# Moving the routing steps, the first expert splits and the expert loads inside the key phase of a cross-attention and expert kernel

## What is computed

```python
x = x + fake_quant_matmul(layernorm(x), ctx)        # L0: quantised product with the context
x = x + moe(layernorm(x))                            # L0: 16 experts, 2 of 16 per token, and a shared pair
x = x + cross_attention(layernorm(x), ctx)           # L1: 32 query heads, 8 key/value heads of 128
x = x + gated_low_rank(layernorm(x))                 # L1: 64 experts of rank 8, 16 of 64 per token

# in moe():
scores = softmax(xt @ router_w + router_b) + router_bias
keep   = the 2 best of 4 groups by their best score
idx    = the 2 best experts among the kept groups
y      = sum over experts of gate[e] * ((silu(xt @ w1 + b1) * (xt @ w2 + b2)) @ w3 + b3)

# in cross_attention():
k = rmsnorm((ctx @ k_proj_w.T) per head); v = ctx @ v_proj_w.T    # k and v depend on ctx alone
```

## Time and profile before

| quantity | value |
|---|---|
| time, median of 3 executions | 661.31 us |
| lowest and highest of them | 659.51 and 673.06 us |
| the profiled execution (one of the three) | 673.06 us |
| its span, first to last instruction | 671.2 us |
| busy PE, DVE, ACT, POOL | 575.7, 458.4, 352.6, 366.9 us |
| chain that ended last: PE, POOL, DVE | 39%, 18%, 15% of the span |
| mean granted clock of TensorE | 0.954 |

### The profile page before, as it was taken

The page is one execution under the profiler, slowest core; times in us unless marked ns, Lnnn a source line. Parts: engine busy times, 40 slices in busy tenths (PEclk is TensorE's granted clock), DMA queues, the critical chain, the costliest instruction groups (busy, mean ns, idle before and its releaser), DMA issues.

```text
span 671.2 us, 11710 instructions
## 1 busy us (share of the span) xinstructions
PE 575.7 (86%) x3255; PEld 280.2 (42%) x3255; DVE 458.4 (68%) x1066; ACT 352.6 (53%) x792; POOL 366.9 (55%) x396
## 2 busy tenths in 40 slices
PE   2949967678676994999996899999999969999997
PEld 1414523376554443444441344444444424444453
DVE  6898698847777476555557999999999920000773
ACT  4336623546555404757566677777777723133132
POOL 5960137859898460678785444444545414368011
PEclk9979977879999996999998999999999979999999
DMA  9993027789987650487759999999999993324001
GB/s 343 408 372 132 17 49 195 149 277 329 361 285 255 217 176 1 109 196 181 204 111 200 180 171 179 179 184 178 180 184 177 179 160 118 125 73 178 1 1 63
DMA packets 211846, 118.78 MB, mean 177 GB/s; under 512 B 188497, under 2 KB 196817, under 8 KB 208866
## 3 DMA queue, kind: packets, MB, share of 16 engines
q1 hardware_dynamic: 209346, 108.58, 62.9%
q0 software_dynamic: 2288, 9.70, 4.7%
q10 hardware_dynamic: 176, 0.04, 0.0%
HBM read 56.94 MB, written 15.20 MB: 107 GB/s over the span
## 4 chain that ended last, share of the span: by engine, by line
PE 39%; POOL 18%; DVE 15%; issue 11%; SPq 7%; DMA 6%; ACT 3%; POOLq 0%; DVEq 0%; ACTq 0%
PE ps L345 12%; PE ps L347 12%; PE ps L346 12%; SPq L499 7%; POOL wsp L1292 6%; POOL hlr L1292 4%; POOL q_sb L1292 3%; DVE q_sb L1554 2%; PE ps L526 1%; POOL q_sb L1309 1%; DVE f32r L1707 1%; DMA stage<-in_moe,disp 1%; POOL hsp L1292 1%; DVE x_sb L1810 1%; DMA stage<-in_first_chunks 1%
## 5 line engine op out<-in xcount | busy, mean ns | idle before, releaser
L1292 POOL TENSOR_TENSOR wsp<-stage,wsp 128x512 f16<-128x512 f32 (+1 forms) x69 | 78.1, 1157 | 63.3 <-ACT wsp L1135 63.2
L1162 ACT ACTIVATE f32r<-f32r,mneg 128x512 f32<-128x512 f32 x128 | 91.4, 715 | 29.7 <-DVE mneg L1832 29.6
L1832 DVE CUSTOM_DVE_ANT_0 f32r<-ps,nmask 128x512 f32<-128x512 f32 x128 | 82.5, 680 | 1.9
L1427 POOL TENSOR_SCALAR hlr<-f32r,rinv 128x512 f16<-128x512 f32 x64 | 45.1, 714 | 47.6 <-DVE rinv L1837 45.9
L1427 POOL TENSOR_SCALAR stage<-f32r,rinv 128x512 f16<-128x512 f32 x64 | 43.6, 691 | 46.4 <-DVE rinv L1837 46.3
L1292 POOL TENSOR_TENSOR hlr<-f32r,hlr 128x512 f16<-128x512 f32 x36 | 41.2, 1155 | 48.1 <-ACT hlr L1244 33.5
L345 PE MATMUL ps<-q_sb 128*128 128x512 f16 x132 | 53.3, 404 | 15.5 <-POOL q_sb L1292 11.8
L1694 DVE TENSOR_REDUCE ss<-f32r 128x4 f32<-128x512 f32 x48 | 32.8, 684 | 47.1 <-ACT f32r L1045 47.0
L345 PE MATMUL ps<-k_sb,q_sb 128*128 (+1 forms) x128 | 49.4, 386 | 11.5 <-DVE mneg L1832 8.8
L346 PE MATMUL ps<-q_sb 128*128 128x512 f16 x132 | 53.2, 403 | 0.0
L347 PE MATMUL ps<-q_sb 128*128 128x512 f16 x132 | 52.7, 399 | 0.0
(11 more groups left out here) (363 smaller groups left out, 1539.7 us busy)
## 6 DMA issues: line engine op xcount, KB each, us to landing
stage<-in_wq SPq DMA_DIRECT2D x8, 1024.0 KB, 5.0
stage<-in_wo SPq DMA_DIRECT2D x8, 1024.0 KB, 4.7
q_sb<-in_moe SPq DMA_DIRECT2D x9, 768.0 KB, 7.6
xs_dram<-zeros SPq DMA_DIRECT2D x1, 5888.0 KB, 29.2
pT<-xs_dram SPq DMA_DIRECT2D x23, 256.0 KB, 6.2
r_dram<-f32r SPq DMA_DIRECT2D x23, 256.0 KB, 6.0
stage<-in_moe SPq DMA_DIRECT2D x6, 768.0 KB, 8.7
k_sb<-in_wkv SPq DMA_DIRECT2D x3, 1024.0 KB, 19.0
```

The lines of the kernel that those rows point to most:

```text
L1162: act.activation(f32r[:, j % 4, :], f32r[:, j % 4, :], ACT.Exp, bias=mneg[:, j % 4:j % 4 + 1], scale=-1.0, accum_out=psum_col[:, j % 4:j % ...
L1292: return pool.tensor_tensor(dst_lo, src, dst_hi, ALU.subtract)
L1427: pool.tensor_scalar(halves(j)[:, 0, :], f32r[:, j % 4, :], rinv[:, 0, j % 4:j % 4 + 1], PSCALE, ALU.mult, ALU.mult).then_inc(s_ph, 1)
L1832: dve.tensor_tensor_reduce(f32r[:, j % 4, :], ps[j % 4][:, :], nmask[:, qt, :], 0.125, BIG, ALU.add, ALU.min, mneg[:, j % 4:j % 4 + 1]).th ...
```

## The change

Five moves, and one size. (1) POOL makes the low halves of experts 0 and 1 and of the bias directly before the key phase instead of at tiles 11 to 15. (2) POOL's scatters stand at tiles 9 to 12 instead of 6 to 9. (3) PE's `positions` stands at tile 8 instead of 6, DVE's `slot_numbers` at 6 instead of 5 and `owners_and_gates` at 9 instead of 8. (4) SP loads experts 5, 2, 3 and 4 after the transposes of tiles 3 to 6 instead of before the phase, and experts 6 and 7 after tiles 7 and 8 instead of after tile 15. (5) SP loads the first four token blocks after tile 12 instead of 11. The size is `dynamic_dma_scratch_size`, the bytes of each SBUF partition set aside for the descriptors of POOL's DMAs, 1024 instead of 4096.

```diff
@@ sync
-            load_expert(5)
-            sp.wait_ge(s_cq, BATCH)
-            load_expert(2)
-            load_expert(3)
-            sp.wait_ge(s_vp, NST)
-            load_expert(4)
...
             for r in range(2 * NST):
                 k_transpose(r)
-                if r == 11:
+                if r == 3:
+                    load_expert(5)
+                if r == 4:
+                    sp.wait_ge(s_cq, BATCH)
+                    load_expert(2)
+                if r == 5:
+                    load_expert(3)
+                if r == 6:
+                    sp.wait_ge(s_vp, NST)
+                    load_expert(4)
+                if r in (7, 8):
+                    load_expert(r - 1)
+                if r == 12:
                     sp.wait_ge(s_disp, 1)
                     sp.wait_ge(s_sct, 16 * 2 * NT)
                     for n in range(4):
                         load_slots(n)
-            for n in (6, 7):
-                load_expert(n)
@@ tensor, beside_keys
-                if j == 6:
+                if j == 8:
                     positions()
@@ gpsimd
+            w12_lo(0)
+            w12_lo(1)
+            for n in range(2):
                 pool.wait_ge(s_w3h, n + 1)
                 low(split_at(n, 1, W3), landed_at(n, W3), split_at(n, 0, W3)).then_inc(s_w3p, 1)
-            def beside_keys(r):
-
-                if 6 <= r < 10:
-                    scatters(r)
-                elif r in (11, 13):
-                    w12_lo((r - 11) // 2)
-                elif r in (12, 14):
-                    w3_lo((r - 12) // 2)
-                elif r == 15:
-                    pool.wait_ge(s_b3h, 1)
-                    low(b3[1], b3s[0:E_ROUTED + 1, :], b3[0]).then_inc(s_b3l, 1)
+            pool.wait_ge(s_b3h, 1)
+            low(b3[1], b3s[0:E_ROUTED + 1, :], b3[0]).then_inc(s_b3l, 1)
...
-            rms_phase(0, 2, 8, pT2, None, beside_keys)
+            rms_phase(0, 2, 8, pT2, None, {r: scatters for r in (9, 10, 11, 12)})
@@ vector
-            rms_phase(0, 2, 8, True, {3: scores_of_experts, 4: gates, 5: slot_numbers, 8: owners_and_gates, 12: gates_turned})
+            rms_phase(0, 2, 8, True, {3: scores_of_experts, 4: gates, 6: slot_numbers, 9: owners_and_gates, 12: gates_turned})
@@ kernel
-    nc = bacc.Bacc("TRN2", target_bir_lowering=False, num_devices=1, dynamic_dma_scratch_size=4096)
+    nc = bacc.Bacc("TRN2", target_bir_lowering=False, num_devices=1, dynamic_dma_scratch_size=1024)
```

More of the change, by code:

```diff
@@ L1324, in w12_lo @@
                 last.then_inc(s_w12l, 1)
-            def w3_lo(n):
+            w12_lo(0)
+            w12_lo(1)
+            for n in range(2):
                 pool.wait_ge(s_w3h, n + 1)
                 low(split_at(n, 1, W3), landed_at(n, W3), split_at(n, 0, W3)).then_inc(s_w3p, 1)
-            def beside_keys(r):
-                if 6 <= r < 10:
-                    scatters(r)
-                elif r in (11, 13):
-                    w12_lo((r - 11) // 2)
-                elif r in (12, 14):
-                    w3_lo((r - 12) // 2)
-                elif r == 15:
-                    pool.wait_ge(s_b3h, 1)
-                    low(b3[1], b3s[0:E_ROUTED + 1, :], b3[0]).then_inc(s_b3l, 1)
+            pool.wait_ge(s_b3h, 1)
+            low(b3[1], b3s[0:E_ROUTED + 1, :], b3[0]).then_inc(s_b3l, 1)
             def scatter(k, t):
@@ L1348, in scatters @@
             def scatters(r):
-                if r == 6:
+                if r == 9:
                     pool.wait_ge(s_idx, 1)
                     pool.wait_ge(s_zero, 16)
-                for t in ((0, 1), (2, 3))[r % 2]:
-                    scatter((r - 6) // 2, t)
+                if r >= 9:
+                    for t in ((0, 1), (2, 3))[r % 2]:
+                        scatter((r - 9) // 2, t)
             def rms_phase(r0, iters, tiles, parts, quarter=None, beside=None):
@@ L1368, in body @@
                                 quarter(i, j // 4, c)
-                        if beside:
-                            beside(tiles * i + j)
+                        if beside and tiles * i + j in beside:
+                            beside[tiles * i + j](tiles * i + j)
                 body(0, True)
```

## The result

The changed kernel is slower by a little: 664.04 us median of 12 executions, beside 660.26 us of 12 of the kernel before on the same chip. The ratio is 1.0070, 95% interval 1.0047 to 1.0094, so +4.6 us (3.1 to 6.2). The forecast was 660.5, that is -0.8: the number lies in the range, the sign is wrong.

A forecast was written before the change was run, and what follows sets the result against it. It took POOL's backlog, then SP's rate of issue, then token block 4's landing as the bound. Costs taken at zero and 0.8 us left of PE's 3.7 us idle gave -0.8 us: 661.31 to 660.5 us, range 653 to 671.

The forecast's parts named there:

- The descriptor space, taken at zero: POOL's indirect DMAs: with about three in flight, the smaller space was to cost nothing.
- a rival (0.03, 695 us): Space too small for two POOL DMAs at once, so each waits for the last to land; 695 us, chance 0.03.
- The early low halves, taken at zero: Ahead of the key phase: POOL's subtractions from 53.0 to 60.8 us delay DVE's normalisation 2.3 us, covered, so no cost.
- The prediction's cover of 2.02 + 2.2 us: DVE's 2.02 us wait for ACT's high halves and 2.2 us before PE's transposes were to hide the normalisation's delay.
- the prediction's own upper bound of 3.6: Largest cost of the early low halves if DVE's earlier work is shut out too: 7.8 - 4.2 = 3.6 us.
- SP's rate of issue: End of the key phase: after POOL's backlog, SP's queue bounds, with key transposes 1.29 us each.
- The count moved to tile 8: Key phase: PE's wait moves from tile 6 to 7, up to 6.1 us; slots are known 5.5 us later.
- The expert loads, "cost nothing in their new place": Experts 5, 2, 3 and 4 among the key transposes: zero cost, 7 us of buffers against a load's 6.3.
- The landing of block 4: Token block 4, with nothing ahead in SP's queue, lands in 3 us instead of 6.34, at 144.3 us.
- PE's arrival there: At token block 4: PE comes 2.9 us later, because block 2 waits for tile 14's transposes to leave its buffer.
- The prediction's gain: At token block 4: 0.8 us left of PE's 3.7 us idle time, carried through the expert stage one to one.
- the rival "the phase gets longer": Lower-clock tiles, full owners' step, uncovered normalisation, unshortened landing; two or three give +2 to +8, about 666 us; chance 0.22.

The follow-up runs named there:

- b_early: The kernel before with only the seven early low halves moved ahead of the key phase; +2.5 us (0.9 to 4.1).
- b_2048: The kernel before with 2048 bytes of descriptor space instead of 4096; +0.7 us (-1.2 to 2.6).
- b_1024: The kernel before with 1024 bytes of descriptor space instead of 4096, nothing else changed; +2.2 us (0.7 to 3.9).
- b_swap: The kernel before with the loads of experts 6 and 7 issued behind token block 4's load, not ahead of it; -4.3 us (-5.9 to -2.7).
- b_early_tiles: The kernel before with early low halves and later tiles for count, slots, owners, scatters and token blocks; expert loads and space as before; +3.8 us (2.1 to 5.5).
- a_4096: The changed kernel with the descriptor space back at 4096 bytes, nothing else undone; +2.2 us (0.6 to 3.9) against the kernel before.
- b_early_loads: The kernel before with early low halves and expert loads among the key transposes; scatters, count, token blocks and 4096 bytes as before; +4.3 us (2.2 to 6.5).
- b_512: The kernel before with 512 bytes of descriptor space instead of 4096; one execution, 664.17 us.

## Why the prediction was wrong

- **The descriptor space, taken at zero: failed.** The prediction counted about three DMAs in flight and let the wait begin at the second as a rival (0.03, 695 us). The number in flight doesn't decide for the scatters: in 1024 bytes seven go out, and the eighth waits for the youngest, though the first had long landed. Nor is it the count alone, since eight fetches in the same space don't wait; the rule stays open. The wait costs 6.79 us on POOL, +2.4 us of time in the changed kernel and +2.2 in the kernel before. Both ends of the term were mis-read: not zero, and not 35 us.
- **The early low halves, taken at zero: failed.** The prediction's cover of 2.02 + 2.2 us existed only behind the 14.40 us; without these the two waits are absent, the stream begins at 47.87 us instead of 53.0 and meets the normalisation in full. It delays the phase by 3.7 us (2.2 to 4.9 over all pairs of profiles), so the prediction's own upper bound of 3.6 had the right size. Time: +2.5 us. The 7.8 us that leave POOL's part of the chain at 117 us bought nothing in b_early, since SP's rate of issue, which the prediction named as the next bound, was the bound already.
- **The count moved to tile 8: right, to 0.8 us or better.** PE idle up to 6.1 us, measured 5.37; tile 7 in 5.1 us at the lower level, measured 4.9 (84.01 to 88.92, granted clock 0.50 to 0.53, 1.2 GHz); DVE's wait 3.7, measured 3.67; owners' step 5.5, measured 4.8 (98.37 to 103.21); a low half with two scatters 3.6, measured 3.62 (109.36 to 112.98).
- **The expert loads, "cost nothing in their new place": failed in the trace, open in the time.** The prediction set buffers of four tiles against a load's 6.3 us. Scatters landed in 7.9 us instead of about 3.5, single key transposes in up to 11.1 instead of 4.7 (b_2048). ACT's 3.69 us for a transpose's buffer lie under POOL's gap in the changed kernel; with 4096 bytes ACT waits 3.37 and 3.90 us for such buffers, and DVE 2.47 behind it. Because the scatters landed late, the full descriptor space cost 6.79 us here and 3.22 in b_1024: the terms that were taken at zero are not independent.
- **The landing of block 4: right; PE's arrival there: mis-sized.** The block landed in 2.9 us, forecast 3, and PE's wait went to 0.47 us. The prediction's gain was what is left of PE's 3.73 us after PE comes 2.9 us late. The wait to be had was larger, 5.51 us in b_2048, and worth 4.3 us of time in b_swap. But PE came far later than 2.9 us: it turns the first blocks 14.7 us late (132.39, beside 117.73 in b_2048) and is 6.1 us late at block 4 (142.19, beside 136.07); with 4096 bytes it is 1.8 late there (137.88). So by block 4 the stage has made up 8.6 of the 14.7 us, 5.0 of them from the wait that is gone (5.51 to 0.47), and at the marker 4.4 are left.
- **Where the sum went wrong in place.** The prediction's positions carry the 11.1 us of the long operation. Without them block 4 should have gone out at 141.3 - 11.1 = 130.2 us; it went out at 139.27, 9 us later. The phase starts 3.2 us later (67.08, 63.84 in b_2048). From there to the issue of the first blocks it is 62.4 us, with 4096 bytes 58.9, without the loads as well 54.9 (b_early_tiles): 3.5 us from the space and 4.0 from the loads. The three make 10.7; the steps in between came out a little shorter than forecast.

By parts, in time: early low halves +2.5, later tiles +1.3, loads -1.6 (from +3.8 to the 2.2 of a_4096), space +2.4; the sum is 4.6 by construction, up to rounding. Only the first has an interval of its own, which excludes zero, and b_1024 gives the last one's size a second time, with another such interval; the middle two are differences within the uncertainty, and b_early_loads, 1.8 above b_early, speaks against the sign of the third. So the two steps that are shown to have failed are the two terms at zero, the descriptor space and the early low halves; their 2.5 and 2.4 us come to the whole loss. The outcome is that of the rival "the phase gets longer", +2 to +8 us, of whose four causes only the uncovered normalisation showed: the clock was granted at 1.00 from 100 to 116 us, the owners' step took 4.8 us, and the landing shortened.

## What to carry to other kernels

Look for waits whose length depends on chance before using one as cover: if the profiled execution lies 12 us above the median, find the row that holds them first. Before making the descriptor space smaller, run it alone and read POOL's gaps at each indirect DMA: neither the number in flight nor the number in a row foretold them here. When a transfer at the end of a phase is late, ask what stands ahead of it in its queue before moving anything into the phase: two lines in another order gained 4.3 and 4.4 us, five moves and the smaller space lost 4.6.

## What the runs showed of the hardware

- An operation of DVE that meets a run of POOL's subtractions may wait for one of them or for all. The same pair gave 2.17 us in fifteen profiles and 14.40 in three. The four short steps at 51 us waited up to one subtraction each (0.90 to 1.08 us) in all five profiles that have seven subtractions there. By the Trainium skill (SBUF — State Buffer, SBUF: two separate sides) an operation of POOL, or one of DVE that needs the ports the two share, keeps them for its whole instruction once it has started; the short steps agree with that (the last three are 0.04 to 0.06 us short of one subtraction), and the 14.40 us do not, unless POOL wins every time anew.
- Three scatters of 128 rows fit in 512 bytes of descriptor space, seven in 1024, at least eight in 2048. The one that found none went out 0.5 to 0.6 us after the landing of the scatter just before it (b_512 twice, changed kernel). Fetches differ: with 512 bytes every second one from the fourth on waited, for the last but one, and with 1024 bytes none of eight waited.
- Six loads of 768 KB among the transposes raised the mean busy share of the DMA engines at 100 to 120 us from 0.65 (b_2048) to 1.08 (changed kernel), and the median landing of a scatter from 3.5 to 7.9 us. Two such loads just ahead of a token block in SP's queue made it land in 7.7 us instead of 2.9 (b_2048, b_swap).
- What follows the marker, the same program in all kernels, takes 434.4 to 439.2 us, by the profile. PE's granted clock there isn't the same either: between 540 and 560 us it was 0.87 in b_1024 and 1.00 in the changed kernel.
